# Running each routed expert on the rows that chose it, instead of on every row: one decoder layer on one Trainium2 core

## The reference, cut to what matters

```
scores = sigmoid(x3 @ router.T)                    # (4096, 16)
sc = scores + e_bias                               # 4 groups of 4 experts; the 2 best groups stay,
tidx = the 4 best experts of those groups          # and of these the 4 best experts, for each row
tw = 2.5 * scores[tidx] / sum(scores[tidx])
mlp_e(x) = (silu(x @ gate_e.T) * (x @ up_e.T)) @ down_e.T      # 256 -> 128 -> 256
routed = sum over the 4 chosen e of tw_e * mlp_e(x3)
shared = mlp of two more experts that every row uses
out = layernorm(x3 + routed + shared)
```

## Time and profile before

| | |
|---|---|
| runs, us | 2091.45, 2090.27, 2094.7 (median 2091.45) |
| profiled execution | span 2090.7 us from its first to its last instruction; no time of its own is given beside the span, which lies inside the three runs |
| PE, DVE, ACT, POOL busy | 1873.8, 1517.0, 912.3, 434.4 us |
| `experts` | from 1442.5 us to the end: 648 us |
| mean granted TensorE clock | 0.948 of full speed |

### The profile page before, as it was taken

How to read it: one execution, slowest core, us unless ns; L and a number is a source line. 1 busy time by engine, 2 the same in 40 slices (tenths; PEclk the granted TensorE clock), 3 DMA queues, 4 the chain that set the end, 5 groups by cost and what they waited for, 6 DMA issues and landing times. The chain is left out here.

```text
span 2090.7 us, 38064 instructions
## 1 busy us (share of the span) xinstructions
PE 1873.8 (90%) x13184; PEld 1192.7 (57%) x13184; DVE 1517.0 (73%) x3864; ACT 912.3 (44%) x1398; POOL 434.4 (21%) x616
## 2 busy tenths in 40 slices
PE   6969899997887799899899999766799999999997
PEld 4646676775554233333333333244688788888886
DVE  7954454554897788788778888184988877777776
ACT  5534454553322166566556666512323223332322
POOL 2143343311332411111111111362500000000000
PEclk9989999998998599999999999988999999999999
DMA  5798576661596643434435330575200000000000
GB/s 168 224 183 145 98 122 105 106 165 48 179 249 193 87 70 52 86 58 62 79 56 72 69 55 26 160 230 179 56 31 1 31 31 1 31 31 1 21 11 11
DMA packets 146279, 187.31 MB, mean 90 GB/s; under 512 B 48002, under 2 KB 112098, under 8 KB 141502
## 3 DMA queue, kind: packets, MB, share of 16 engines
q1 hardware_dynamic: 120606, 139.93, 27.3%
q0 software_dynamic: 9552, 30.43, 9.7%
q10 hardware_dynamic: 15952, 14.63, 2.8%
HBM read 114.33 MB, written 70.20 MB: 88 GB/s over the span
## 5 line engine op out<-in xcount | busy, mean ns | idle before, releaser
L1460 ACT ACTIVATE sa_prob<-sa_ps_s 128x1024 f32<-128x1024 f32 (+3 forms) x480 | 376.2, 825 | 280.0 <-PE sa_ps_s L1369 202.1
L1518 DVE CUSTOM_DVE_ANT_0 sa_ps_m<-sa_ps_m,sf_later 128x282 f32<-128x282 f32 (+4 forms) x640 | 278.4, 460 | 53.4 <-PE sa_ps_m L1342 52.2
L1521 DVE TENSOR_REDUCE sa_piece_max<-sa_ps_m 128x1 f32<-128x512 f32 x384 | 259.0, 687 | 45.1 <-PE sa_ps_m L1342 44.5
L1859 DVE SCALAR_TENSOR_TENSOR mo_acc<-mo_ps_o,mo_keep,mo_acc 128x256 f32<-128x256 f32 x512 | 212.2, 476 | 71.7 <-PE mo_ps_o L274 71.5
L1342 PE MATMUL sa_ps_m<-sa_k,sa_q 96*128 96x512 bf16 (+4 forms) x768 | 210.2, 334 | 21.2 <-DVE sa_max_parts L1549 7.4
L1725 ACT ACTIVATE mo_h_hi<-mo_h 128x512 fp32r<-128x512 f32 x144 | 91.0, 632 | 272.7 <-DVE mo_h L1841 270.5
L1496 POOL TENSOR_SCALAR_AFFINE_SELECT sa_prob<-sa_prob 128x256 f32<-128x256 f32 x256 | 102.2, 406 | 500.1 <-ACT sa_prob L1460 497.6
L1342 PEld LDWEIGHTS sa_ps_m<-sa_k,sa_q 96*128 96x128 bf16 x768 | 66.4, 99 | 240.9 <-issue 109.8
L734 DVE TENSOR_TENSOR la_att<-la_ps_att,lf_cap 128x512 f32<-128x512 f32 x128 | 88.3, 690 | 110.3 <-PE la_ps_att L642 110.3
L272 PE MATMUL mo_ps_o<-mh_lo,mo_h_hi 128*128 128x256 f32 x576 | 162.5, 282 | 1.1 <-DVE mo_h_lo L1845 0.9
L274 PE MATMUL mo_ps_o<-mh_hi,mo_h_hi 128*128 128x256 f32 x576 | 163.0, 283 | 0.0
(11 more groups left out here) (222 smaller groups left out, 3855.5 us busy)
## 6 DMA issues: line engine op xcount, KB each, us to landing
la_q<-s_q_parts POOLq DMA_DIRECT2D x72, 128.0 KB, 6.0
la_k<-s_k_parts POOLq DMA_DIRECT2D x72, 128.0 KB, 8.0
sa_q<-s_q_parts SPq DMA_DIRECT2D x72, 128.0 KB, 5.1
sa_k<-s_k_parts SPq DMA_DIRECT2D x66, 128.0 KB, 7.0
s_y<-la_y SPq DMA_DIRECT2D x16, 512.0 KB, 3.6
s_x<-cl_xn SPq DMA_DIRECT2D x16, 512.0 KB, 6.1
s_y<-sa_y SPq DMA_DIRECT2D x16, 512.0 KB, 3.2
mw_raw<-experts SPq DMA_DIRECT2D x18, 384.0 KB, 4.0
```

Source lines behind the costliest of these rows:

```text
L1460: nc.scalar.activation(dst, src, ACT.Exp, scale=HD ** -0.5).then_inc(expd[s], 1)
L1518: nc.vector.tensor_tensor_reduce(ps_m[:, s, 0:hi - lo], ps_m[:, s, 0:hi - lo], later[:, BANK + lo - first:BANK + hi - first], 1.0, -BIG, A ...
L1521: nc.vector.tensor_reduce(piece_max[:, j, t, n:n + 1], ps_m[:, s, 0:hi - lo], AX.X, ALU.max).then_inc(piece_done[s], 1)
L1859: last = nc.vector.scalar_tensor_tensor(acc[:, t], ps_o[:, s, t], keep[:, n * TB + t, i - 1:i], acc[:, t], ALU.mult, ALU.add)
```

## The change

`experts` is replaced by two stages, and softmax attention gets a small extra job.

1. **Zeros.** The lists of rows, `xs`, lie in HBM: NLIST = 144 blocks of 128 rows (the 16,384 chosen pairs of row and expert, and room for partly filled blocks). In softmax attention DVE clears one tile of 128x2048, and in the last batch row SP writes it 18 times (1 MB each) over `xs`.
2. **`share_and_place`.** PE runs the two shared experts on all 8 tiles (16 `gate_up`, 8 `project_down` of 24 matmuls); DVE adds x3 and SP stores the sum in `shared`. DVE routes in six calls (for 4, 8, 8, 4, 4 and 4 blocks): `choose` is the old `route` up to the chosen experts, `weigh` the weights, and `place_tokens` gives each chosen row its place in its expert's list, from counts that PE makes with bf16 matmuls (`count`). POOL then writes each block of 128 rows to its 4 experts' lists by 128 indirect DMAs. DVE also takes over the remainders of the last 12 experts' weights from POOL.
3. **`routed_experts`.** 72 pairs of list blocks pass through PE: transpose, gate and up with the rows as the stationary operand (so the 256 columns of gate and up of one half are one matmul), silu, transpose, down. `turn_x` is 4 transposes, `gate_up` 12 matmuls of 256 columns, `turn_h` 2 transposes and `project_down` 6 matmuls of 256 columns; three passes as before. Which expert a block belongs to is a register that PE loads from SBUF, four of them for two pairs. SP loads the lists and stores the results in `ys`; POOL gathers, for each tile, 4 results for each row by 16 indirect DMAs; DVE weighs and adds them (`combine`) and does the layer norm.

The core of the diff (long parts of `choose` that equal the old `route`, allocations and the host's layout of the tables are left out):

```diff
@@ softmax_attention
         # DVE, at the start
+            nc.vector.memset(zero[:, :], 0.0).then_inc(zero_set, 1)
         # SP
             def batch_row(b, last):
+                if last:
+                    sp.wait_ge(zero_set, 1 + START)
                 for g in range(QUADS):
                     if not (last and g == QUADS - 1):
                         maxima(*after(b, g))
                     if last:
+                        for i in range(g * ZERO_RUNS // QUADS, (g + 1) * ZERO_RUNS // QUADS):
+                            sp.dma_start(io["xs"].rearrange("(p n) c -> p (n c)", p=P)[:, i * ZERO_RUN:(i + 1) * ZERO_RUN],
+                                         zero[:, :]).then_inc(zeroed, 16)
                         for e in range(g * W_SLOTS // QUADS, (g + 1) * W_SLOTS // QUADS):
                             weights.load(sp, io, e)
+            sp.wait_ge(zeroed, 16 * ZERO_RUNS)
@@ experts, replaced by share_and_place
+def route_ahead_of(n):
+    return {0: (0, 1), 1: (2,), 3: (3,), 4: (4,), 5: (5,)}.get(n, ())
+ROUTE_TILES = ((0, 1), (1, 3), (3, 5), (5, 6), (6, 7), (7, 8))
+def pairs_for(tile):
+    last = [hi for lo, hi in ROUTE_TILES if lo <= tile < hi][0]
+    return min(PAIRS, -(-(last * TB * TOPK + EXPERTS - 1) // 2))
+        # PE
+            for n in range(NT):
+                for g in route_ahead_of(n):
+                    count(g)
+                gate_up(n * SHARED)
+                if n:
+                    project_down(n - 1)
+                gate_up(n * SHARED + 1)
+            project_down(NT - 1)
+        # DVE
+            for n in range(NT):
+                for g in route_ahead_of(n):
+                    choose(g)
+                    weigh(g)
+                    place_tokens(g)
...
+                for k in range(n * SHARED, (n + 1) * SHARED):
+                    gated(k)
+                    if (e := next(w_next, None)) is not None:
+                        weights.remainder(dve, nc.vector, e)
+                    if n and k == n * SHARED:
+                        add_up(n - 1)
+                if n + 2 < NT:
+                    split_x(n + 2)
+        # POOL
+            def scatter(n):
+                pool.wait_ge(x_in[n], 16)
+                for t in range(TB):
+                    for i in range(TOPK):
+                        rows = places.row[:, n * TB + t, i:i + 1]
+                        nc.gpsimd.indirect_dma_start(io["xs"], bass.IndirectOffsetOnAxis(ap=rows, axis=0), x[:, n % X_SLOTS, t], None).then_inc(scattered[n], 16)
+            for g, (lo, hi) in enumerate(ROUTE_TILES):
+                pool.wait_ge(placed, g + 1)
+                for n in range(lo, hi):
+                    scatter(n)
+                    if n and n - 1 + X_SLOTS < NT:
+                        pool.wait_ge(scattered[n - 1], TB * TOPK * 16)
+                        pool.wait_ge(added, n)
+                        load_x(pool, n - 1 + X_SLOTS)
@@ routed_experts
+        # SP
+            for q in range(PAIRS):
+                if q + SLOTS < PAIRS:
+                    load_rows(q + SLOTS)
+                sp.wait_ge(y_done, q + 1)
+                sp.dma_start(io["ys"][list_rows(q)].rearrange("(s p) c -> p s c", p=P), y[:, q % SLOTS]).then_inc(y_out[q % SLOTS], 16)
+        # PE
+            def gate_up(q):
+                if q % (LOADED // 2) == 0:
+                    _, found = nc.values_load_multi_w_load_instructions(
+                        places.first[0:1, 2 * q:2 * q + LOADED], engines=(mybir.EngineType.PE,), min_val=0, max_val=(ALL_EXPERTS - 1) * EXPERT_W)
+                    for i, value in enumerate(found):
+                        first[2 * q + i] = nc.tensor.snap(value)
+                pe.wait_ge(x_split, q + 1)
+                if q >= 2:
+                    pe.wait_ge(multiplied, q - 1)
+                for s in range(2):
+                    tokens = slice(s * P, (s + 1) * P)
+                    for a in range(CT):
+                        at = bass.ds(first[2 * q + s] + a * C, C)
+                        hi, lo = w_hi[:, at], w_lo[:, at]
+                        out = ps_gu[:, q % 2, s * C:(s + 1) * C]
+                        nc.tensor.matmul(out, x_lo[:, q % 2, a, tokens], hi, start=a == 0, stop=False)
+                        nc.tensor.matmul(out, x_hi[:, q % 2, a, tokens], hi, start=False, stop=False)
+                        last = nc.tensor.matmul(out, x_hi[:, q % 2, a, tokens], lo, start=False, stop=a == CT - 1)
+                last.then_inc(gu_ps, 1)
+            for q in range(PAIRS):
+                if q + 2 < PAIRS:
+                    turn_x(q + 2)
+                if q + 1 < PAIRS:
+                    gate_up(q + 1)
+                turn_h(q)
+                if q:
+                    project_down(q - 1)
+        # ACT
+            for q in range(PAIRS):
+                if q + 2 < PAIRS:
+                    round_x(q + 2)
+                if q + 1 < PAIRS:
+                    activate(q + 1)
+                round_h(q)
+                if q:
+                    take_y(q - 1)
+        # POOL
+            for n in range(NT):
+                for s in range(SLOTS):
+                    pool.wait_ge(y_out[s], -(-(pairs_for(n) - s) // SLOTS) * 16)
+                for i in range(TOPK):
+                    if n:
+                        pool.wait_ge(combined, (n - 1) * TOPK + i + 1)
+                    for t in range(TB):
+                        at = places.row[:, n * TB + t, i:i + 1]
+                        nc.gpsimd.indirect_dma_start(picked[:, i, t], None, io["ys"][0:pairs_for(n) * COLS], bass.IndirectOffsetOnAxis(ap=at, axis=0)).then_inc(gathered[i], 16)
+                root(n)
+        # DVE
+            for q in range(PAIRS):
+                if q + 2 < PAIRS:
+                    split_x(q + 2)
+                if q + 1 < PAIRS:
+                    multiply(q + 1)
+                split_h(q)
+                closing(q)
```

More of the change, by code:

```diff
@@ new lines, in share_and_place @@
+        g1, g2, g3, gsum, gge = (ph.sb(n, [P, MOST_BLOCKS, GROUPS]) for n in ("g1", "g2", "g3", "gsum", "gge"))
+        wsum = ph.sb("wsum", [P, MOST_BLOCKS])
+        counts = [ph.sb(f"counts{i}", [P, EXPERTS]) for i in range(2)]
+        held = [ph.sb(f"held{i}", [P, EXPERTS]) for i in range(2)]
+        whole = ph.sb("whole", [P, EXPERTS], I32)
+        before, base, gap, none_new = (ph.sb(n, [P, EXPERTS]) for n in ("before", "base", "gap", "none_new"))
+        earlier = [ph.sb(f"earlier{i}", [P, EXPERTS]) for i in range(2)]
@@ L1657, in _, with count @@
                     load_xT(n + 2)
[L1658 to L1662, removed]
-            sp.wait_ge(stored, 16 * NT)
+                for e in (next(later_weights, None), next(later_weights, None)):
+                    if n and e is not None:
+                        weights.load(sp, io, e)
+                    elif e is not None:
+                        weights.load(sp, io, e)
+                sp.wait_ge(added, n + 1)
+                sp.dma_start(io["shared"][tile_rows(n)].rearrange("(n p) c -> p n c", p=P), acc[:, n % 2]).then_inc(acc_out[n % 2], 16)
+            for half in range(2):
+                sp.wait_ge(acc_out[half], NT // 2 * 16)
         @blk.tensor
         def _(pe):
+            def count(g):
+                n = (ROUTE_TILES[g][1] - ROUTE_TILES[g][0]) * TB
+                out = ps_rank[:, g % 2, 0:(n + 1) * EXPERTS]
+                kinds = kept_b[:, :, :].rearrange("p n e -> p (n e)")
+                pe.wait_ge(kept_done, g + 1)
+                nc.tensor.matmul(out, every[:, :], kinds[:, 0:(n + 1) * EXPERTS], start=True, stop=False, skip_group_check=True)
+                for m in range(2, n + 1):
+                    nc.tensor.matmul(out[:, m * EXPERTS:], every[:, :], kinds[:, EXPERTS:(n + 2 - m) * EXPERTS],
+                                     start=False, stop=False, skip_group_check=True)
+                nc.tensor.matmul(out[:, 0:n * EXPERTS], until[:, :], kinds[:, EXPERTS:(n + 1) * EXPERTS],
+                                 start=False, stop=True, skip_group_check=True).then_inc(rank_ps, 1)
             def gate_up(k):
-                n, e = divmod(k, ALL_EXPERTS)
+                n, e = divmod(k, SHARED)
                 s = k % 2
@@ L1695, in project_down @@
                 last.then_inc(o_ps, 1)
[L1697 to L1698 removed]
+            pe.wait_ge(ranks_cast, 3)
             for n in range(NT):
[L1700 to L1707 removed]
+                for g in route_ahead_of(n):
[4 more added lines that the diff above has]
+                gate_up(n * SHARED + 1)
@@ new lines, in _ @@
+            project_down(NT - 1)
+            pe.wait_ge(tables_in, 48)
+            pe.wait_ge(fresh_done, N_ROUTES)
+            for s, rows in enumerate((fresh, fresh_end)):
+                last = nc.tensor.transpose(ps_rank[0:FRESH, s, 0:P], rows[:, :, :].rearrange("p g e -> p (g e)"), ident[:, :])
+            last.then_inc(fresh_ps, 1)
+            pe.wait_ge(spans_done, 1)
```

(27 more changed lines are left out.)

641 lines of the change are left out of this document (410 added, 231 removed).

## The result

The changed kernel took 2110.14 us (median of four runs, 2096.8 to 2114.82), the kernel before, beside it on the same chip, 2090.86: a ratio of 1.0086 [1.0053, 1.0119], 0.9% slower, where 4.5% faster was predicted. It lies outside the forecast of 1960 to 2040 us and inside the wide range of 1930 to 2120. The profiled execution is the fastest of the four, 2096.8 us with a span of 2095.1.

The account below looks back on a forecast made before the run. PE was taken to bound experts, its matmul steps 602 of 648 us. 1442.5 + 12 zeros + 212 share and place + 276 pairs + 12 gather waits + 42 tail = 1996.5, so 1997 us (−4.5%); forecast 1960 to 2040, wide range 1930 to 2120.

Parts of the forecast that it names:

- p: Time of one pair of list blocks in routed_experts, set by the slowest engine; taken as 3.7 us, between 3.0 and 4.6.
- Prices of the pair: Engine work for one pair in routed_experts: PE 3.0 us, DVE 2.6, ACT 2.0; imperfect overlap expected, so 3.7 was taken.
- Transfers: SP's 0.75 MB for a pair in routed_experts: 3.0 us at 249 GB/s, 4.1 at 182.
- The register load: PE's expert addresses in routed_experts: 0.6 us of sequencer and 1.0 of loading for a pair, nothing if hidden.
- Low clock: Rival, chance 0.06: PE's small gaps in the pairs keep its clock at 1.2 GHz; pair 5.9 us, time 2143 us.
- Indirect DMAs: POOL's 256 scatters and gathers, priced at 1.2 us each; rival, chance 0.18: at 2.1 us each the time is 2170 us.
- Share and place: The share_and_place stage: 212 us, DVE busy most of it and POOL's last scatter level with DVE's end.
- Zeros: Eighteen 1 MB writes on SP's queue in softmax attention's last batch row delay its end; +12 us, up to 19.
- Waits for gathers: In routed_experts, DVE waits for POOL's gathers at tiles 2, 4, 5 and 6, some 3 us each; +12 us.
- The tail: After the last pair, the uncovered combine of tiles 6 and 7, with 16 gathers, layer norm and store; 42 us.
- PE's sequencer: Rival, chance 0.15: PE's sequencer, with its expert address registers, bounds the pairs; p = 4.6 us, time 2054 us.
- the prediction's own warning: Prediction is wrong above all if an indirect DMA takes over 1.7 us, or a pair in routed_experts over 5.

Follow-up runs that it names:

- Run 1: Changed kernel with SP issuing the load of pair q+6 where it issued that of q+4, nothing else changed; 2010.99 us, ratio 0.9611 to the kernel before.
- run 9: Kernel with early row load, late root and x loaded by SP, plus the zero writes in three quads instead of four; 1953.39 us, ratio 0.9381.

## Why the prediction was wrong, step by step

- **The step that failed**: "The orders on PE, ACT and DVE leave each product an iteration to arrive, so the slowest engine sets p." It holds for these three and leaves out the fourth order, SP's, which stands in the diff: the load of pair q+4 comes behind the wait for the product of pair q−1 (`take_y`, at the end of iteration q), and the rows are wanted at the head of iteration q+2. One iteration, 2.76 us on PE, should hold 0.6 of `take_y`, 0.4 of the store's issue, 2.9 until the rows land. The four row slots looked like a lead of four pairs; the order left one. Run 1 undid this alone, and the time became 2011 us against 1997. That p became 3.69 there, the 3.7 of the prediction, is luck: it was 2.76 up to the first gather and 3.96 behind it, where the prediction had 3.7 throughout and 12 us of waits for gathers. The pair was priced too high, the waits too low, and the two nearly cancel.
- **Prices of the pair**: PE's 3.0 us was 2.76 once it ran free, and the 0.7 added because "engines this close to each other never overlap fully" was not needed: PE was busy 42 of 42 us. Transfers were no bound. The register load was priced at 0 to 1.6 us for a pair; up to the first gather it is worth 4.92 − 3.83 = 1.09 in the starved loop and 0.01 in a fed one.
- **Low clock** was a rival with 0.06. It came, at 0.82, but as a consequence: PE stood for 2.4 us in two pairs (1.26 for rows, 1.13 for registers), and with the rows early the granted clock was 1.00 up to the first gather with nothing else changed. Its price was not small: from 1671 to 2044 us 1,730 matmuls kept PE busy for 268 us, 0.155 each, against 42.00 / 369 = 0.114 in run 1's opening. By that some 70 us of the pairs' time (an estimate) are matmuls at the lower clock, more than the 55 that PE waited for rows after the first pair.
- **Indirect DMAs**, the rival with 0.18, fell: the median is 0.96 us for a scatter and 0.95 for a gather, with 0.30 to the next, 1.26 against the 1.2 taken. By instruction, with the shortest, the median and the longest in ns:

```profile
L1825 POOL DMA_INDIRECT s_xs<-ms_x,mp_row x128: 956/960/2025, 1466.1 to 1658.7; - x128
...
L2206 POOL DMA_INDIRECT mo_picked<-s_ys,mp_row x128: 942/952/1225, 1759.6 to 2080.0; - x128
```

  The 0.55 us of a direct one plus 6 ns for each of 128 descriptors gave 1.3, near the measured one. That its two parts are right is not shown. The 6 ns came from loads at different times: POOL's were issued at 676.9 to 729.7 us, in slices of 193 and 87 GB/s, SP's at 817.1 to 1211.2, in slices of 52 to 86, so their later landing can also be traffic.
- **Share and place** was 223 us against 212. DVE was done at 1644.6, 197 us into the stage; POOL ended it, with its last scatter at 1658.65. POOL's wait for the first sum (11.8 us) ended at 1521.37, 74 us into the stage where the prediction had 84. From there it had 96 × 1.2 + 10 = 125 us, and 149 passed: 6 because a scatter took 1.26, 0.7 and 6.6 in later waits for `added` and 10.9 of landing and barrier where 10 stood for both, and the rest in further loads of x and longer scatters.
- **Zeros**: 12 predicted, 5 in this execution, where the closing stage, which began 12.7 us late (1356.11 against 1343.46), caught up 8. In the ten other profiled executions with the zeros in their old place the new stage began at 1452.5 to 1460.4, 10 to 18 us late. So the size fits and the profiled execution happens to show less of it; that the zeros are all of this delay is not shown (run 9).
- **Waits for gathers**, predicted at tiles 2, 4, 5 and 6, were 15.6 us in five places up to the last store of `ys`, against 12, since slow pairs gave the gathers time. In run 1 they were 47.7 us up to that store and 72.7 with the tail: six pairs of 2.76 us are 17 us, not 22, and POOL's chain needs 28 for a tile. **The tail** was 51 us against 42 (the terms named there add to 40.9): the sum took tile 6 to be summed 5 us after the loop's end, but its gathers began only at 2032.08, behind the root of tile 5 at 2030.85, and ended at 2051.1, 7 us after the last store of `ys`. With the late root the tail was 42 (1927.3 to 1969.1).
- **Rivals**: none had SP's order. "PE's sequencer" came nearest in p, with 4.6, and "low clock", with 5.9, named a part of what was seen; the prediction's own warning, a pair over 5 us, is what happened.

## What to carry to other kernels

Count the lead of a load in the order in which its queue issues it, not in buffers: find the wait that stands ahead of it on that queue, and what that wait is for. A store and a prefetch on one in-order queue tie the next input to the last output; moving the prefetch's index by two took 99 us from this kernel without a byte of memory. In this starved loop the small costs (four registers in one load, the clock) showed at full price and went with the starvation, so undo the wait first and price the rest after. The next bound then shows itself: here POOL's gathers, which slow pairs had hidden.

## What the runs showed of the hardware

Some scatters took up to 2.02 us instead of 0.96. Two of them in the timeline of the changed kernel with what DVE did then, and ahead of them one beside another kind of DVE instruction:

```profile
1494.33 0.68 DVE L1949 TENSOR_TENSOR ms_h<-ms_silu,ms_ps_u 128x512 f32<-128x512 f32 x1
1494.55 0.98 POOL L1825 DMA_INDIRECT s_xs<-ms_x,mp_row  x1 [0.30 <-issue]
...
1497.39 1.23 DVE L1944 TENSOR_TENSOR ms_x_lo<-ms_xT,ms_x_hi 128x1024 fp32r<-128x1024 f32 x1
1497.54 1.91 POOL L1825 DMA_INDIRECT s_xs<-ms_x,mp_row  x1 [0.30 <-issue]
...
1558.30 0.96 DVE L1617 TENSOR_TENSOR mh_lo<-mr_raw,mh_hi 128x768 fp32r<-128x768 f32 x1
1558.58 1.51 POOL L1825 DMA_INDIRECT s_xs<-ms_x,mp_row  x1 [0.30 <-issue]
```

In these two, where DVE subtracts two operands that both lie in SBUF, the scatter ends 0.83 us after DVE does (1497.39 + 1.23 + 0.83 = 1499.45 and 1558.30 + 0.96 + 0.83 = 1560.09, each the end of the scatter to 0.01). Beside a product that reads PSUM (L1949) it took 0.98, near its usual 0.96. The Trainium skill ("SBUF — State Buffer", section "SBUF: two separate sides") says that DVE and GpSimd share a pair of ports under an exclusive lock, which a DVE instruction with two SBUF inputs holds for its whole length against a GpSimd one that reads SBUF; an indirect DMA that reads its row numbers there would be such a one. The trace agrees in kind. The price is small here: a scatter's mean is 1.03 us against a median of 0.96, 9 us for all 128, where the prediction, going by that page, put it at some 2.5 us for each that meets the right DVE instruction.
